# Last output tile of a graph layer with layer norm: x and its bias added in PSUM by two identity products

## The reference

```
relevance = sum(hi_t * hj_t)            # hi_t, hj_t: linear in x and in the edge type's embedding
A = softmax(where(adj, relevance, -1e9))
hidden = relu((A @ x) @ gcn_w + gcn_b)
y = x + hidden @ Wo_w + Wo_b
out = (y - mean(y)) / sqrt(var(y) + 1e-5)
```

## Time and profile before

| | us |
|---|---|
| median of three runs | 373.4 |
| lowest and highest | 372.9, 373.54 |
| the profiled execution | 373.2 |
| its span, first to last instruction | 371.3 |
| PE busy | 364.5 (98% of the span) |
| DVE busy | 274.7 (74%) |
| ACT busy | 181.5 (49%) |
| POOL busy | 145.1 (39%) |

### The profile page before, as it was taken

The page is one execution under the profiler, slowest core; times in us unless marked ns, Lnnn a source line. Parts: engine busy times, 40 slices in busy tenths (PEclk is TensorE's granted clock), DMA queues, the critical chain, the costliest instruction groups (busy, mean ns, idle before and its releaser), DMA issues.

```text
span 371.3 us, 9946 instructions
## 1 busy us (share of the span) xinstructions
PE 364.5 (98%) x3827; PEld 316.8 (85%) x3827; DVE 274.7 (74%) x776; ACT 181.5 (49%) x374; POOL 145.1 (39%) x108
## 2 busy tenths in 40 slices
PE   8999999999999999999999999999999999999994
PEld 5688898988889898888989889898988989898894
DVE  1579778687786868788686777858677786877956
ACT  1576717164372715527272561816347181625574
POOL 1513551716134171513517152261714327141814
PEclk9999999999999999999999999999999999999998
DMA  7996014464443556354365524435553444550033
GB/s 221 352 327 200 24 29 170 158 187 156 139 145 96 173 169 184 116 158 162 89 182 169 179 94 155 160 118 184 169 160 108 129 159 149 171 171 4 2 127 132
DMA packets 43412, 55.48 MB, mean 149 GB/s; under 512 B 10368, under 2 KB 37632, under 8 KB 43392
## 3 DMA queue, kind: packets, MB, share of 16 engines
q1 hardware_dynamic: 42592, 54.44, 46.3%
q10 hardware_dynamic: 800, 0.77, 0.6%
HBM read 42.61 MB, written 12.58 MB: 149 GB/s over the span
## 4 chain that ended last, share of the span: by engine, by line
PE 95%; DMA 2%; DVE 1%; SPq 1%; ACT 0%; issue 0%; POOL 0%
PE banks L471 28%; PE banks L473 27%; PE banks L472 27%; PE banks L531 7%; PE banks L497 7%; DMA xt_sb<-in_x_t_dram 2%; DVE m_lo L920 0%; SPq L398 0%; ACT xt_hi L749 0%; PE banks L616 0%; DVE stats L871 0%; DVE xt_sb L866 0%; SPq L394 0%; POOL rstd L1239 0%; ACT xt_sb L832 0%
## 5 line engine op out<-in xcount | busy, mean ns | idle before, releaser
L1171 POOL TENSOR_TENSOR y_sb<-y_sb,wob_sb 128x1536 f32<-128x1536 f32 x15 | 52.8, 3522 | 88.0 <-DVE y_sb L888 73.9
L783 ACT CAST z_hi<-banks 128x512 fp32r<-128x512 f32 x48 | 26.6, 588 | 96.6 <-PE banks L531 90.8
L866 DVE TENSOR_TENSOR y_sb<-banks,y_sb 128x384 f32<-128x384 f32 x60 | 33.4, 556 | 47.3 <-PE banks L473 43.7
L472 PE MATMUL banks<-wo_lo,hs_hi 128*128 128x384 f32 x180 | 60.5, 336 | 0.0
L471 PE MATMUL banks<-wo_hi,hs_hi 128*128 128x384 f32 x180 | 60.5, 336 | 0.0
L473 PE MATMUL banks<-wo_hi,hs_lo 128*128 128x384 f32 x180 | 60.5, 336 | 0.0
L471 PE MATMUL banks<-z_hi,gcn_hi 128*128 128x512 f32 x144 | 58.3, 405 | 0.0
L471 PE MATMUL banks<-xt_hi,m_hi 128*128 128x512 f32 x144 | 57.1, 397 | 0.5 <-DVE u_sb L922 0.5
L473 PE MATMUL banks<-xt_hi,m_lo 128*128 128x512 f32 x144 | 56.5, 392 | 0.0
L473 PE MATMUL banks<-z_hi,gcn_lo 128*128 128x512 f32 x144 | 56.5, 392 | 0.0
L472 PE MATMUL banks<-z_lo,gcn_hi 128*128 128x512 f32 x144 | 56.1, 390 | 0.0
(11 more groups left out here) (108 smaller groups left out, 614.7 us busy)
## 6 DMA issues: line engine op xcount, KB each, us to landing
x_sb<-in_x_dram SPq DMA_DIRECT2D x16, 768.0 KB, 4.7
xt_sb<-in_x_t_dram SPq DMA_DIRECT2D x15, 768.0 KB, 6.4
y_sb<-in_x_dram SPq DMA_DIRECT2D x15, 768.0 KB, 4.5
out_dram<-y_sb SPq DMA_DIRECT2D x30, 384.0 KB, 2.5
adj_sb<-in_adj_dram SPq DMA_DIRECT2D x32, 64.0 KB, 3.0
xt_sb<-in_x_t_dram SPq DMA_DIRECT2D x2, 384.0 KB, 7.1
xt_sb<-in_x_dram SPq DMA_DIRECT2D x1, 768.0 KB, 6.2
w2t_sb<-in_w_t_dram SPq DMA_DIRECT2D x3, 192.0 KB, 4.6
```

The source lines that it names most:

```text
L472: pe.matmul(acc, a_hi, b_lo, start=False, stop=False)
L783: act.copy(by_graph(z_hi[:, f, :]), mixed(f)).then_inc(zhi, 1)
L866: dve.tensor_tensor(y_home(g, slot)[:, q, :], out_bank(g, q)[:, 0:HID], y_home(g, slot)[:, q, :], ALU.add).then_inc(added, 1)
L1171: pool.tensor_tensor(y_home(g, slot), y_home(g, slot), wob_sb[:].rearrange("p (o n) -> p o n", o=1).to_broadcast([P, PAIRS, HID]), ALU.add ...
```

## The change

The last tile no longer has its sum made by VectorE. Ahead of its nine matmuls TensorE puts x with its bias into the bank, by two products with the identity: one of the rounded part (end_hi), one of the rest (end_lo). So the bank holds the whole y when the ninth matmul ends. VectorE takes its statistics from the bank, and both halves of the last tile are read from the bank when they are normalised. ScalarE's centring pass and VectorE's last pass read the same bank, so VectorE waits for the centring.

```diff
 (tensors)
+        ident_r = sb("ident_r", [P, P], F32R)
+        end_hi = sb("end_hi", [P, HID], F32R)
+        end_lo = sb("end_lo", [P, HID], F32R)
...
 (TensorE, out)
+                end = static(g, LAST) and q == PAIRS - 1
+                if end:
+                    pe.wait_ge(ident_r_ready, 1)
+                    pe.wait_ge(end_lo_ready, 1)
+                    pe.matmul(out_bank(g, q)[:, 0:HID], ident_r[:], end_hi[:], start=True, stop=False)
+                    pe.matmul(out_bank(g, q)[:, 0:HID], ident_r[:], end_lo[:], start=False, stop=False)
                 for n, c in enumerate(BLOCKS):
                     mm = three(out_bank(g, q)[:, 0:HID], high[:, c, ts], low[:, c, ts], wo_hi[:, c, :], wo_lo[:, c, :],
-                               n == 0, n == C - 1)
+                               n == 0 and not end, n == C - 1)
...
 (ScalarE, body of the last group)
                     split_z(g)
+                    act.wait_ge(xb, GROUPS)
+                    act.copy(end_hi[:], y_home(g, par)[:, PAIRS - 1, :]).then_inc(end_hi_ready, 1)
                     normalise_last(LAST - 2, 1, 1, (0, 1))
...
 (ScalarE, the end)
             act.wait_ge(nmean_ready, 1)
-            act.activation(end, end, ACT.Identity, bias=nmean[:, 0:1]).then_inc(centred, 1)
+            act.activation(end, out_bank(LAST, PAIRS - 1)[:, SHARE:HID], ACT.Identity, bias=nmean[:, 0:1]).then_inc(centred, 1)
...
 (VectorE, before the first group)
             row_products(0, 0)
+            dve.tensor_copy(ident_r[:], ident[:]).then_inc(ident_r_ready, 1)
...
 (VectorE, the end)
-            for q in range(PAIRS):
+            for q in range(PAIRS - 1):
                 residual(LAST, 1, q)
                 dve.wait_ge(statd, PAIRS * LAST + q + 1)
                 moments(LAST, (q,))
+            total = out_bank(LAST, PAIRS - 1)[:, 0:HID]
+            dve.wait_ge(out_mm, PAIRS * GROUPS)
+            dve.bn_stats(stats[:, PAIRS - 1, :], total).then_inc(statd, 1)
+            dve.wait_ge(statd, PAIRS * GROUPS)
+            moments(LAST, (PAIRS - 1,))
...
+            dve.wait_ge(centred, 1)
             dve.wait_ge(rstd_ready, LAST + 5)
-            dve.tensor_scalar(end[:, 0:SHARE], end[:, 0:SHARE], mv[:, at, 0:1], rstd[:, at:at + 1],
+            dve.tensor_scalar(end[:, 0:SHARE], total[:, 0:SHARE], mv[:, at, 0:1], rstd[:, at:at + 1],
                               ALU.subtract, ALU.mult).then_inc(y_ready, 1)
...
 (GpSimd, body of the last group, between its two halves)
+                        if h == 0:
+                            pool.wait_ge(end_hi_ready, 1)
+                            pool.tensor_tensor(end_lo[:], y_home(g, par)[:, PAIRS - 1, :], f32(end_hi[:]),
+                                               ALU.subtract).then_inc(end_lo_ready, 1)
```

More of the change, by code:

```diff
@@ L278, in gnn_layernorm_kernel @@
         veps_end = sem("veps_end")
+        ident_r_ready = sem("ident_r_ready")
+        end_hi_ready = sem("end_hi_ready")
+        end_lo_ready = sem("end_lo_ready")
         nmean_ready = sem("nmean_ready")
```

## The result

| | us |
|---|---|
| before, median of 6 runs | 373.12 |
| with the change, median of 6 runs | 374.75 |
| ratio, with its 95% interval | 1.0044 [1.0031, 1.0058] |
| with the change, lowest and highest | 374.25, 375.28 |
| its profiled execution, and its span | 374.98, 373.2 |

The change makes the kernel 1.6 us slower, where 0.1 us faster was forecast, and the time lies outside the range.

A forecast was written before the change was run, and what follows sets the result against it. The chain through TensorE's last product, VectorE, GpSimd and ScalarE's last store was taken to bound the end: -0.60 add, +0.35 products, 0.13 of 0.25 us lost in a handover, giving 373.4 - 0.12 = 373.3 us; range 372.7 to 373.9.

The forecast's parts named there:

- landed at 370.64: Kernel end: ScalarE's last store, issued at 368.84, lands 1.8 us later, 0.12 us earlier than before.
- the new wait: Last tile: VectorE's last pass now waits for ScalarE's first; both last passes start at 368.32, losing 0.13 of 0.25 us.
- the fetch of code: Given as an example of something outside the priced cases, shifted by added instructions; chance 0.07, shared between both signs.
- identity products: TensorE, ahead of the last tile's nine: two products at 0.174 us each, 0.35 us at full price.
- TensorE pays more: Rival: a 0.20 us step on TensorE at the change of weights to the identity; gain 0.05, time 373.35; chance 0.14.
- full 32-bit products: Rival: identity products run as full 32-bit, 1.30 us in place of 0.35; end 0.70 later, 374.1; chance 0.02.
- Statistics from the bank: VectorE, last tile: statistics read from a bank take 0.56 us, no change, and start at 366.56 instead of 366.81.
- ScalarE's queue is late next: ScalarE's first pass over the last tile still starts at 367.94, held by the third tile's pass; lasts 0.35 us.
- Full gain: Rival: ScalarE's first pass does not hold back the two last passes; gain 0.25 us, time 373.15; chance 0.06.
- the lower bound: VectorE's last pass, 256 columns from a bank: 0.42 us at the lower end, 0.55 us taken.
- The preparations: Copies of identity and x, and GpSimd's 0.9 us subtraction, fit idle stretches before the last tile; costed at nothing.
- VectorE's half ends last: Rival, kernel end: VectorE's last store lands over 1.86 us after issue and ends the kernel; 373.45 to 373.65; chance 0.19.

The follow-up runs named there:

- a_nogen: Changed kernel without the general path on any engine, so no flag read and no branch; 373.07 us, ratio to before 1.0006.
- b_nogen: Kernel before the change, without the general path on any engine, so no flag read and no branch; 373.0 us, ratio 1.0007.
- a_mid: Changed kernel with one filling of 225 unused columns on VectorE ahead of the comparison that makes the flag; 372.84 us, ratio 1.0.
- a_early: Changed kernel with the general path's flag made early: transpose at 356.0, comparison at 357.4; 372.88 us, ratio to before 1.0001.
- a_pe3: Changed kernel with three idle 384-column full 32-bit products on TensorE between its transpose and its flag read; 374.87 us, ratio 1.0055.

## Why the prediction was wrong

The step that failed is the last of the sum, "landed at 370.64": the time from issue to landing was taken from the earlier trace rows as a constant of the store. In the runs here it is 1.8 to 2.1 where the fetch of 16 KB does not stand ahead of a part of the store, and 3.3 to 3.9 where it does. With the change it was 3.9, and the 2.1 us are more than all other terms together. The place at which it had to be seen is the paragraph on the new wait. It names the flag of the general path and costs what follows it at nothing. It did not follow the branch to what it starts, although the flag was on the path of what moved. The prediction gave 0.07 to "the fetch of code", shared between both signs, as something that added instructions shift, and named no packet; the table of the DMA queues of the kernel before, asked for the last microsecond, would have shown one (its start is 370.471 in the trace).

The prediction says that a time outside its range would mean that something moved ahead of the last tile. Nothing did: the last tile's first product starts at 364.33, against 364.45. What moved lies behind the tile.

Point by point, with 0.12 us added to the times of the changed kernel:

- The identity products cost 0.17 each. First product to first product of the nine: 364.68 - 364.33 = 0.35, as said. The rival "TensorE pays more" and the one of full 32-bit products fall.
- Statistics from the bank take 0.56 and start at 366.56, as said. The power ends at 368.17 (367.50 + 0.55 + 0.12), as said: the 0.25 us up to there are real.
- ScalarE's queue is late next, as said: its first pass starts at 367.93 (said 367.94), though its input is 0.24 earlier, and lasts 0.35. "Full gain" falls.
- VectorE's last pass starts at 368.31 (said 368.32), right behind `centred`, and lasts 0.54 (said 0.55; from SBUF 0.41). The slower reading of a bank was the right choice against the 0.42 of the lower bound. The rule of the Trainium skill cited there, in "VectorE: DVE Perf Modes", section "Mode 2×_2P", fits this number.
- ScalarE's last pass starts at 368.37, where 368.32 was said: 0.05 more, which no run explains. So its store is issued 0.07 earlier than before, not 0.12. With VectorE's at no change, the instructions' gain is at most 0.07 us; a_nogen and b_nogen don't resolve it.
- Three sums are a little off, and none changes the outcome. By the terms given the range would be 372.8 to 374.0 (373.4 - 0.25 - 0.35 and 373.4 + 0.24 + 0.35), not 372.7 to 373.9, and 374.75 lies outside both. ScalarE's lower bound is 0.31, not 0.30, and VectorE's pass comes to 0.56, not 0.55.
- The preparations cost nothing. GpSimd's subtraction took 1.02 us from 353.98, not 0.9, still 9.3 us before TensorE asks for it.
- The rival "VectorE's half ends last" had the right question, how long a store takes to land, at the wrong store: VectorE's landed in 1.8 us.

The page "Runtime: NRT & Kernel Launch" of the Trainium skill, section "Instruction fetch mechanics", says that code comes in blocks of 16 KiB over a DMA queue that the engine's sequencer drives, and that a taken branch makes it fetch the target's block when that is not at hand. The traces agree on the size (16384 bytes), and that a packet follows the branch. The page calls the cost of crossing from one block to the next mostly hidden; here TensorE doesn't wait for the packet (its next instruction, the DRAIN at the program's end, starts at 369.26 and the packet at 370.14), and the cost falls on a store that has nothing to do with it.

## What to carry to other kernels

The end of a kernel isn't over with its last instruction: look at what the DMA engines have to do between the last store's issue and its landing, code included, and at who triggers it. An edit that moves a flag or a branch earlier moves a 16 KB transfer with it; where that may meet the last store, hold the branching engine on a semaphore of the last pass (one line, 1.6 us here). A change of 0.1 us in a tail can cost 1.6 us by changing an order (0.08 us of delay gave it all back in a_mid), so the order of transfers is to be read as well as their lengths.

## What the runs showed of the hardware

- A fetch of 16 KB of code occupies one DMA engine for 1.0 to 1.6 us (that packet near the end of the kernels run here: 1.02 to 1.59). A store of another queue whose share on that engine comes behind it waits for it: 1.8 becomes 3.3 to 3.9 us. In each of the four traces with the loss, eight of the store's 128 packets and one completion start only as the fetch ends.
- It starts 1.19 to 1.42 us behind TensorE's branch over code that is not run, in nine kernels; 1.67 in a_mid.
- In nine of the ten traces with the branch (all but a_early, where the fetch is long over) its place against the last store's issue goes with who waits: with the branch 0.03 us ahead of the issue the store waits (a_pe3), with it 0.04 behind it doesn't (a_mid).
- TensorE reads a value and branches before the products that stand ahead of it have run (a_early: read at 362.72, branch at 363.66, last product from 365.65 to 365.99); three idle products held neither (a_pe3: read at 368.35, products to 368.93).
